# Spreading the queries of a vision tower's first attention by one VectorE operation

## The reference

```python
h = tokenizer(x)                                   # shifted copies, layernorm, projection to 192
h = h + attn0(layernorm(h))                        # the part that changes
h = h + attn1(layernorm(h))                        # qk-norm, gated heads of 64
h = h + attn2(layernorm(h))                        # l2-norm over the heads, heads of 64
h = h + ffn(layernorm(h))                          # relu, top-k mask by image

def attn0(x):                                      # 12 heads of 16
    qkv = einsum('bnhd,hde->bnhe', x.reshape(b, n, 12, 16), W_qkv) + b_qkv
    q, k, v = split(qkv, 3)
    p = softmax(einsum('bihd,bjhd->bhij', q, k) / sqrt(192))
    return einsum('bhij,bjhd->bihd', p, v).reshape(b, n, 192) @ W_out + b_out
```

## Time and profile before

| | |
|---|---|
| median of 3 runs | 1573.12 us (1569.11 to 1573.88) |
| the profiled execution's own time | 1564.85 us |
| its span in the profile | 1562.7 us |
| TensorE busy over the span | 82% |
| VectorE, ScalarE, GpSimdE busy | 64%, 60%, 29% |
| phase A | 0 to 186 us |
| phase B | 186 to 458 us |
| phases C and D | 458 to 1190 us |
| selection and feed-forward | from 1190 us |

### The profile page before, as it was taken

The page is one execution under the profiler, slowest core; times in us unless marked ns, Lnnn a source line. Parts: engine busy times, 40 slices in busy tenths (PEclk is TensorE's granted clock), DMA queues, the critical chain, the costliest instruction groups (busy, mean ns, idle before and its releaser), DMA issues.

```text
span 1562.7 us, 27926 instructions
## 1 busy us (share of the span) xinstructions
PE 1282.7 (82%) x9582; PEld 1164.6 (75%) x9582; DVE 999.2 (64%) x2455; ACT 943.8 (60%) x3298; POOL 458.7 (29%) x447
## 2 busy tenths in 40 slices
PE   1688777778768999999977999999984128999999
PEld 0387776667757888898966888888872117999998
DVE  5663255544546999999866788888875773333333
ACT  2445177777855889889875888888873102222233
POOL 0132100210203233233203334343413304555555
PEclk9688899899977999999998999999996558999999
DMA  5130100020000000000000000000002100000000
GB/s 233 59 117 1 51 12 1 1 62 1 1 1 1 2 1 1 2 1 2 2 10 1 2 1 2 2 1 1 2 2 81 61 0 1 10 1 10 10 10 12
DMA packets 7040, 30.09 MB, mean 19 GB/s; under 512 B 1603, under 2 KB 4400, under 8 KB 5560
## 3 DMA queue, kind: packets, MB, share of 16 engines
q1 hardware_dynamic: 6902, 28.31, 5.6%
HBM read 26.54 MB, written 1.77 MB: 18 GB/s over the span
## 4 chain that ended last, share of the span: by engine, by line
PE 39%; DVE 24%; ACT 4%; issue 3%; POOL 1%; POOLq 0%; ACTq 0%; DVEq 0%
PE bank L1344 4%; DVE t_ss L734 4%; DVE f_eq L1625 4%; DVE t_p L772 3%; PE bank L1370 3%; PE bank L1332 2%; DVE t_raw L750 2%; DVE t_ss L731 2%; PE bank L1312 2%; PE bank L1689 2%; PE bank L1691 2%; PE bank L1704 2%; PE bank L1692 2%; PE bank L1690 2%; PE bank L1693 2%
## 5 line engine op out<-in xcount | busy, mean ns | idle before, releaser
L1164 ACT ACTIVATE t_p<-bank,t_nmax 108x108 f32<-108x108 f32 x792 | 267.4, 355 | 47.6 <-DVE t_nmax L754 46.0
L754 DVE TENSOR_REDUCE t_nmax<-bank 108x4 f32<-108x432 f32 x198 | 119.5, 604 | 141.8 <-PE bank L1344 141.5
L1810 POOL TENSOR_TENSOR f_hid_lo<-f_hid,f_hid_hi 128x432 fp32r<-128x432 f32 (+2 forms) x144 | 145.9, 1014 | 173.5 <-ACT f_hid_hi L1796 173.5
L1013 POOL TENSOR_TENSOR t_sq<-t_raw 108x768 f32<-108x768 f32 x88 | 139.9, 1591 | 181.1 <-ACT t_raw L1104 180.7
L1344 PEld LDWEIGHTS bank<-t_kT,t_qT 128*108 128x108 f32 x1584 | 187.2, 179 | 2.7
L1344 PE MATMUL bank<-t_kT,t_qT 128*108 128x108 f32 x1584 | 187.1, 262 | 0.0
L1766 DVE SCALAR_TENSOR_TENSOR f_hid<-bank,f_maskT 128x432 f32<-128x432 f32 (+2 forms) x144 | 80.2, 557 | 166.9 <-PE bank L1693 165.7
L1796 ACT CAST f_hid_hi<-f_hid 128x432 fp32r<-128x432 f32 (+2 forms) x144 | 73.9, 513 | 182.4 <-DVE f_hid L1766 182.3
L1164 ACT ACTIVATION_READ_ACCUMULATOR t_p<-bank,t_nmax 108x1 f32 x792 | 167.0, 211 | 0.0
L772 DVE TENSOR_TENSOR t_p<-t_p,t_rinv 108x432 f32<-108x432 f32 x198 | 148.9, 752 | 6.8
L1353 PE MATMUL bank<-ident,t_p 108*108 108x108 f32 x792 | 109.6, 261 | 32.6 <-ACT t_xt L1085 28.2
(11 more groups left out here) (224 smaller groups left out, 3487.6 us busy)
## 6 DMA issues: line engine op xcount, KB each, us to landing
A_xraw<-in_x SPq DMA_DIRECT2D x4, 2232.6 KB
A_w<-in_tok_w SPq DMA_DIRECT2D x5, 729.0 KB
f_raw_down<-in_w_proj SPq DMA_DIRECT2D x1, 2304.0 KB, 8.7
out_tokens<-h SPq DMA_DIRECT2D x21, 81.0 KB
f_raw<-in_w_mfc SPq DMA_DIRECT2D x1, 1536.0 KB, 6.9
f_raw<-in_w_mfc SPq DMA_DIRECT2D x2, 768.0 KB, 11.9
W_raw<-in_wC SPq DMA_DIRECT2D x1, 1159.0 KB
W_raw<-in_wC SPq DMA_DIRECT2D x2, 579.5 KB
```

Source lines behind the costliest of these rows:

```text
L754: dve.tensor_reduce(b.nmax[:, 4 * c:4 * c + 4], self.sbank[(3 * g + c) % 2][0:GT, 0:4 * GT].rearrange("p (a n) -> p a n", n=GT), AX.X, ALU ...
L1013: pool.tensor_tensor(b.sq[:, 768 * m:768 * m + 768], v, v, ALU.mult).then_inc(s["sq"], 1)
L1164: act.activation(b.p[g % 2][:, m, :], self.sbank[(3 * g + c) % 2][0:GT, n * GT:(n + 1) * GT], ACT.Exp, bias=b.nmax[:, m:m + 1], accum_out= ...
L1810: pool.tensor_tensor(self.hid_lo[m % 4][:, c], self.hid[m % 4][:, c], self.hid_hi[m % 4][:, c].bitcast(F32), ALU.subtract).then_inc(s["lo" ...
```

## The change

The queries of B are no longer copied by ScalarE in four pieces. One VectorE multiplication per group, `spread_q`, reads the three projected tiles in PSUM, repeats each four times over the slots, and multiplies by a constant `row_of` (1 where the partition belongs to the slot's head, 0 elsewhere), so that the zeros are written anew each time and the two memsets of `qT` go in B. The mask moves into the projections: three of the 16 unused rows of a head carry, on the query side, which image a token belongs to, and on the key side -1e30 for the other images, by constants in `xf` (`image_of`) and in `wB`. The mask matmul goes in B, three per group. The keys' projection and its copy go to the end of the loop body on TensorE and ScalarE, and `norm_root` moves before `exps(g, 1)`. `row_max(g, 2)` goes ahead of `values_in(g+2)`. A wait for an emptied bank counts only the engine that emptied that turn; only `scores` asks for both counts. Two small constants are loaded at the start. C keeps its mask, copies and order; D keeps its order and work, with the new waits.

```diff
+    image_of = fixed("image_of", [GT, GROUP_IMAGES])
+    row_of = fixed("row_of", [128, 4])
...
-        for dst, name in ((ident, "ident"), (owner_f, "owner"), (other_f, "other")):
+        for dst, name in ((ident, "ident"), (owner_f, "owner"), (other_f, "other"), (image_of, "image_of"),
+                          (row_of, "row_of")):
             sp.dma_start(dst[:, :], ins[name]).then_inc(loaded["const"], 16)
...
     def by_vector(self, turn):
-        return self.kind == "D" and turn[0] == "qk" and turn[2] >= 2
+        return turn[0] == "qk" and (self.kind == "D" and turn[2] >= 2 or self.kind == "B" and turn[2] == 0)

-    def evacuated(self, eng, what, g, n=0, before=0):
+    def evacuated(self, eng, what, g, n=0, before=0, and_earlier=False):
         first = self.turned(what, g, n) - before
         if g >= 0 and first > 0:
             late = sum(self.by_vector(t) for t in self.turns[:first])
-            after(eng, self.s["Tev"], first - late)
-            if late:
+            by_vector = self.by_vector(self.turns[first - 1])
+            if and_earlier or not by_vector:
+                after(eng, self.s["Tev"], first - late)
+            if late and (and_earlier or by_vector):
                 after(eng, self.s["kev"], late)
...
+        def spread_q(g):
+            after(dve, s["T"], self.turned("qk", g, 0))
+            after(dve, s["S"], nth(g - 2, 3, 2))
+            src = self.turn_bank("qk", g, 0)[:, 0:3 * GT].rearrange("p (t n) -> p t n", t=3)
+            shape = [128, 3, 4, GT]
+            dve.tensor_tensor(b.qT[g % 2][:, :, :].rearrange("p (t j) n -> p t j n", j=4),
+                              src.unsqueeze(2).to_broadcast(shape),
+                              self.row_of[:, :].unsqueeze(1).unsqueeze(3).to_broadcast(shape),
+                              ALU.mult).then_inc(s["kev"], 1)
...
-        if kind != "D":
+        if kind == "C":
             for k in range(2):
                 dve.memset(b.qT[k][:, :, :], 0.0).then_inc(s["init"], 1)
...
             for k in range(2):
-                dve.memset(b.xf[k][:, 0:384].rearrange("p (t c) -> p t c", c=128)[:, :, 64:65], 1.0)\
+                spare = b.xf[k][:, 0:384].rearrange("p (t c) -> p t c", c=128)
+                dve.memset(spare[:, :, 64:65], 1.0).then_inc(s["init"], 1)
+                dve.tensor_copy(spare[:, :, 65:68],
+                                self.image_of[:, :].unsqueeze(1).to_broadcast([GT, 3, GROUP_IMAGES]))\
                    .then_inc(s["init"], 1)
...
+        if kind == "B":
+            spread_q(0)
         for g in range(GROUPS):
...
             row_max(g, 1)
             gate_step(5)
+            if kind == "B" and more:
+                spread_q(g + 1)
             weigh(g, 0)
...
+            row_max(g, 2)
             if kind == "B" and more2:
                 values_in(g + 2)
-            row_max(g, 2)
...
-            if more:
+            if kind != "B" and more:
                 copy_qk(g + 1, 0)
             if before:
                 copy_p(g - 1, 2)
+            if kind == "B" and g + 5 < GROUPS and g:
+                norm_root(g + 5)
...
-            if kind == "B" and more:
-                copy_qk(g + 1, 1)
             if before:
                 copy_o(g - 1, 0)
...
-            if g + 6 < GROUPS:
+            if kind != "B" and g + 6 < GROUPS:
                 norm_root(g + 6)
+            if kind == "B" and more:
+                copy_qk(g + 1, 1)
...
             after(pe, s["exp"], nth(g, 12, 4 * c - 1) - 4)
-            self.evacuated(pe, "qk", g, self.qk_uses - 1)
-            pe.matmul(o[0:GT, 0:4 * GT], self.owner[:, :], self.other[:, :], start=True, stop=True,
-                      skip_group_check=True)
+            self.evacuated(pe, "qk", g, self.qk_uses - 1, and_earlier=True)
+            masked = kind == "B"
+            if not masked:
+                pe.matmul(o[0:GT, 0:4 * GT], self.owner[:, :], self.other[:, :], start=True, stop=True,
+                          skip_group_check=True)
...
-            if kind == "B" and more:
-                turn_qk(g + 1, 1)
             if before:
                 values(g - 1, 0)
...
-            if kind != "B" and more:
-                turn_qk(g + 1, 3)
+            if more:
+                turn_qk(g + 1, self.qk_uses - 1)
...
+    for r in range(GROUP_IMAGES):
+        w[LO + 1 + r, :, 0, :, 16 + r] = 1.0
+        for other in range(GROUP_IMAGES):
+            if other != r:
+                w[LO + 1 + other, :, 1, :, 16 + r] = MASKED
```

More of the change, by code:

```diff
@@ L136, in build_in @@
     shared = attention_buffers(Plan(region), staging_at, weights_at)
-    B = Attention("B", shared, weights=wB, wout=oB, bias=None, **common)
+    B = Attention("B", shared, weights=wB, wout=oB, bias=None, image_of=image_of, row_of=row_of, **common)
     C = Attention("C", shared, weights=splitC, wout=oC, bias=out_bias[:, 0, :], qk_affine=qk_affine, **common)
@@ L168, in _ @@
     def _(pe):
-        pe.wait_ge(loaded["const"], 48)
+        pe.wait_ge(loaded["const"], 80)
         pA.tensor(pe)
@@ L203, in _ @@
         dve.memset(ones[:, :], 1.0).then_inc(pA.ones_set, 1)
-        dve.wait_ge(loaded["const"], 48)
+        dve.wait_ge(loaded["const"], 80)
         dve.tensor_copy(owner[:, :], owner_f[:, :]).then_inc(cast_done, 1)
@@ L625, in __init__ @@
     def __init__(self, kind, buf, weights, wout, bias, nc, sem, bank, h, ident, ones, owner, other,
-                 qk_affine=None, head_scale=None, tail=None):
+                 qk_affine=None, head_scale=None, image_of=None, row_of=None, tail=None):
         self.kind, self.b, self.w, self.wout, self.bias = kind, buf, weights, wout, bias
@@ L632, in __init__ @@
         small = kind == "B"
+        self.image_of, self.row_of = image_of, row_of
         self.rows = 32 if small else 64
@@ L655, in __init__ @@
                  "O h hb kev gate_d gate_a init").split()
-        absent = {"B": "xh xl sq ss norm qn rg hb kev gate_d gate_a", "C": "kev", "D": "rg gate_d gate_a"}[kind].split()
+        absent = {"B": "xh xl sq ss norm qn rg hb gate_d gate_a", "C": "kev", "D": "rg gate_d gate_a"}[kind].split()
         self.s = {n: sem(f"{kind}_{n}") for n in names if n not in absent}
@@ L890, in vector @@
                 dve.memset(b.xf[k][:, :], 0.0).then_inc(s["init"], 1)
[L891 removed]
+            dve.wait_ge(s["init"], 2)
             for k in range(2):
[L893 removed]
+                spare = b.xf[k][:, 0:384].rearrange("p (t c) -> p t c", c=128)
+                dve.memset(spare[:, :, 64:65], 1.0).then_inc(s["init"], 1)
+                dve.tensor_copy(spare[:, :, 65:68],
+                                self.image_of[:, :].unsqueeze(1).to_broadcast([GT, 3, GROUP_IMAGES]))\
                    .then_inc(s["init"], 1)
@@ L1135, in copy_qk @@
             after(act, s["T"], self.turned("qk", g, u))
-            if u == 0:
+            if u == (kind == "B"):
                 after(act, s["S"], nth(g - 2, 3, 2))
@@ L1205, in scalar @@
         for u in range(self.qk_act):
-            copy_qk(0, u)
+            if not self.by_vector(("qk", 0, u)):
+                copy_qk(0, u)
         for g in range(GROUPS + 1):
@@ L1344, in scores @@
                 mm = pe.matmul(o[0:GT, n * GT:(n + 1) * GT], b.qT[g % 2][:, hd, :], b.kT[g % 2][:, hd // self.per_tile, :],
-                               start=False, stop=True, skip_group_check=True)
+                               start=masked, stop=True, skip_group_check=True)
             mm.then_inc(s["S"], 1)
@@ L1907, in full_depth @@
         return np.concatenate([t, np.zeros((128 - GROUP_IMAGES, t.shape[1]), t.dtype)])
+    A["image_of"] = np.repeat(np.eye(GROUP_IMAGES, dtype=f), TOKENS, 0)
+    A["row_of"] = np.repeat(np.eye(4, dtype=f), 32, 0)
     A["owner"] = full_depth(np.repeat(np.eye(GROUP_IMAGES, dtype=f), TOKENS, 1))
```

## The result

The changed kernel takes 1517.0 us (median, 1515.2 to 1518.7) against 1572.1 (1569.1 to 1573.9) measured beside it. The ratio is 0.9651, with a 95% interval of 0.9629 to 0.9673: 3.5% faster. The forecast was 1523, the range 1500 to 1548. The profiled execution took 1515.33 us, with a span of 1513.4; by its own time the forecast was 1515.1. On the medians the gain is 55.1 us and not the 49.8 forecast. The profiled execution of the kernel before was a quick one (1564.85; the timed ones took 1569.11 at the least), so the 5 to 6 us between cannot be placed in the traces.

The account below looks back on a forecast made before the run. No engine bounds phase B; each group is a ring of waits. Savings of 45.1 (19 periods), 5.1 (start of B) and 0.5 (last masks), less 0.9 (loads), give 49.8 us: 1573.12 - 49.8 = 1523.3 us, range 1500 to 1548.

Parts of the forecast that it names:

- The new ring: Waits through TensorE and ScalarE in a plain group of B: 8.75 us a group, against 11.08 before.
- The spread: VectorE's one multiplication of the queries per group, 128x1296 elements: 1.52 us, bounds 1.14 and 1.98.
- The mask: Mask products gone from TensorE's `scores` in B: 0.18 us less per `scores`, bounds 0.10 and 0.28.
- The second ring: Waits through VectorE's spread in a group of B: 8.64 us, 0.11 below the first ring.
- The second ring rules: Rival: the ring through the spread sets B's period, 9.10 to 10.0 us, total 1530 to 1549; chance 0.16.
- The bank waits: Rival: `values` in B still waits for the spread, 0.87 us in 21 groups, 18 us, total 1541; chance 0.07.
- TensorE alone: Rival: TensorE runs back to back in B, 7.5 us a group, 24 us more saved, total 1500; chance 0.11.
- The sum: Whole kernel: 45.1 us saved in 19 periods of B, 5.1 at its start, 0.5 last masks, less 0.9 loads: 49.8.
- cast groups: Groups of B where a weight cast of 2.1 us stands ahead of `copy_x`: 1.0 us more in each of 6.
- VectorE's preparation: A 1.7 us weight operation in B delays the first row maximum: 0.7 us in four groups, 0.2 in two.
- The last three periods: Last groups of B, without `norm_root` but keeping the ring through the spread: 0.5 us less.
- The start of B: Up to the third keys' copy: 5.1 us saved, from memsets 2.2, spread beside keys' copy 0.6, first two groups 2.3.

Follow-up runs that it names:

- constants_later: The changed kernel with the two new small loads issued behind the loads of phase A; 0.9662 of the time of the kernel before.
- both_counts: The changed kernel with reusers of a bank waiting for VectorE's and ScalarE's counts again; 0.9853 of the time of the kernel before.
- norm_root_late: The changed kernel with `norm_root` moved behind `copy_o`, no longer ahead of `exps(g, 1)`; 0.9649 of the time of the kernel before.
- norm_root_last: The changed kernel with `norm_root` put back at the group's end, ahead of the keys' copy; 0.9821 of the time of the kernel before.

## Why the prediction was right

- *The new ring.* 8.75 forecast, 8.72 measured, and in its own steps: none is off by more than 0.1. Each edit undone put back the wait it had been said to remove, at the size of the ring (10.17, 9.65, 9.5, 10.3 us, in groups at full clock). Only the new place of `row_max(g, 2)` was never undone by itself.
- *The spread.* 1.52 forecast, 1.50 measured. The line through 432 and 324 elements carried to 1296.
- *The mask.* 0.18 taken, 0.13 and 0.18 measured.
- *The second ring.* Forecast 8.64, measured 8.30 to 8.39. The slack is three to four times what I gave it, because I summed whole durations: the row maximum gives way after 0.53 of its 0.61 us and the spread after 1.41 of its 1.50. "The second ring rules" was therefore, looking back, less likely than the 0.16 I gave it. The rule of the Trainium skill ("Perfetto Trace Analysis", "Optimizing Scalar/DVE Operations") that smaller instructions may end work sooner was not tried. In this case the trace leaves it nothing to win: the rule is for instructions that cause idle time elsewhere, and 0.33 to 0.42 us of the spread's ring were free.
- *The bank waits.* The rival's price was 18 us for 0.87 a group. The 0.93 measured is right, the 31 us of the stage are not: the clock was missing from my sum.
- *TensorE alone.* It becomes a ring only once `norm_root` is out of the first, and then at 8.39 and not 7.5, since the wait for the third `copy_p` stays.
- *The sum.* Forecast 45.1 for the 19 periods, measured 46.2. The extras were mis-sized both ways: cast groups cost 1.3 more than plain ones, not 1.0; VectorE's preparation 0.58 in three groups, not 0.7, but 2.17 in a fourth, where TensorE waited 1.85 us and half clock followed. The last three periods (8.37, 8.11, 8.05) gave 1.6 and not 0.5, and that covers it. The start of B gave 31.6 - 29.6 = 2.0, not 5.1. That is the initialisation alone, 3.97 to 2.01 us. The first two groups gained nothing: the prologue's projection ran at half clock (2.16 us, before 1.49), and the third copy of the keys comes 17.4 us after the first in both kernels. The end of B gave 3.9 us, partly because the keys' copy now stands later in its group, and not 0.5. A cost 1.7 rather than 0.9, in waits for other loads than the two new ones; it varies by 7 us between traces of the same code, so that it was only 1.7 here is luck. C to E took 1.2 us more rather than nothing. That is not shown to be a cost: constants_later, alike in C to E, took 0.2 us less there than the kernel before. Net 49.3 against 49.8: the good agreement is partly errors of opposite sign, 3.1 too much at the start and 3.4 too little at the end. It holds for this pair of profiled executions; the medians differ by 55.1.

## What to carry to other kernels

Where no engine is full, write the loop as rings of waits, start to start, and look for the second-longest before trusting a gain. The five edits here (spread, mask, place of the keys, place of `norm_root`, bank waits) were worth 52 us in phase B together, but the mask alone nothing and the four others without the spread some 5 us of the launch, because each alone leaves another ring in place. When a change makes TensorE wait longer in one piece, count the clock as well as the wait: a wait of 0.93 us a group cost 1.46. Such a fall can be chance in part, so read it in more than one trace.

## What was unexpected of the hardware

TensorE's clock falls behind single idle times of under 2 us in a loop that is otherwise 80 to 90% busy. Behind 1.94 us (both_counts) and 1.56 us (norm_root_late) it went from 1.00 to 0.50 for some microseconds, though not every time; behind 0.66 us in the plain groups of the changed kernel never. The length of the one wait does not decide it alone: in both_counts 10 of the 19 waits of 1.9 to 2.4 us were followed by a fall, and in the plain groups of norm_root_last, with a wait of 1.57 us each, none. What else decides is not shown here. The Trainium skill ("TensorE: Matmul & The Clock Gate", section "A second HAM failure mode: psum-queue depth-cycling") describes this for another kernel, in bf16: a clock that swings where TensorE idles briefly between groups of products. The traces agree (granted clock 0.58 over 4.11 us behind the 1.94). Filling the idle time with useless products kept the clock at 1.00 from 220 us to the end of the stage, which then took 244.75 us in place of 251.10.
